# A local-attention block: scores behind the value corners, and a new order of work on VectorE

## The chip, the cores and the metric

The kernel runs on one core of a Trainium2 chip, in one launch. The core has TensorE (PE: matmuls into PSUM, eight banks of 512 floats for each of 128 partitions), VectorE (DVE), ScalarE (ACT), GpSimd (POOL), and SyncE (SP), which here issues all DMAs. The engines run side by side, each through its own list of instructions in order, and meet at semaphores. The metric is the device time of one execution in microseconds (us), lower is better. Before the change it is 3746.49 us, the median of three runs (3743.70 to 3751.31).

## The reference

The input x is 8 sequences of 1024 rows of 256 floats. The result is x + A(xn) + F(xn), where xn is x normalised by row, A is a linear attention with a Taylor feature map, and F is a two-layer transformer with local attention. Cut to what matters for F:

```python
for l in range(2):
    h = shift_token(x)                 # second half of the columns comes from the row before
    q, k, v = split(h @ wqkv[l])       # 8 heads of 64
    q = rotary(l2norm(q) * qs); k = rotary(l2norm(k) * ks)
    sim = 8 * q @ k.T                  # blocks of 128 queries, their own 128 keys and the 128 before
    sim = where(i < j or i > j + 128, -max, sim)
    x = x + (softmax(sim) @ v) @ wo[l]
    h = layernorm(shift_token(x)) * lg + lb
    a, g = split(h @ w1[l] + b1[l])
    x = x + (a * gelu(g)) @ w2[l] + b2[l]
```

## The kernel before

The kernel has two parts. `taylor_block` computes xn and A and stores them; it is not changed. `transformer_block`, from about 1020 us on, computes F and adds the rest.

**Tiles and steps.** The 8 sequences are two streams of four. A step is one tile of 128 rows of one stream in one layer. The attention of a tile needs the tile before it in the same stream and layer, so the kernel goes through 32 rounds in which four steps, two streams by two layers, follow each other: 128 steps in 132 slots, and a few more slots to empty the pipeline.

**The slot.** Each engine runs the same sequence of calls, `slot(nxt, cur, att, nrm, ffn)`, once per slot, in which five neighbouring steps stand at five stages: `nxt` gets its rows transposed (`x_T`, `copy_hT`), `cur` is projected to K, Q and V, rotated and transposed, `att` has its attention, `nrm` has its residual x1, its layer norm and the transpose of the result (`hn_T`, `copy_hnT`), and `ffn` goes through the feed-forward (`up`, gelus, `gated`, `down`, `add_ffn`). A step moves on by one stage with each slot. The order within a slot is written out by hand for each engine, and that is what the change edits.

**PE's slot before** (`slot`, line 1458): scores of `att` (lines 1364 and 1371), K and Q of `cur` (1339), `up` (1443, 1448), V (1339), `prob_T` (1382, 1386), `down` (1455), `attend` (values of the middle 1401, of the corners 1411), `heads_T` for K and for Q (1344), `x_T` (1331, 1332), `hn_T` (1427), `out_project` (1420). Scores and corners use 64x64 tiles of the array, the middle values 128x64, all else full 128 wide ones.

**DVE's slot before** (line 1169): `add_attention` (1120, x1 from PSUM), four times `mask_scores` (1091 adds the mask and takes the maximum of a head, 1098 scales the maxima of two), `row_statistics` (1125 on x1, 1127 on its shifted half, 1130, 1132), `normalise` of four heads (1105 reciprocal, 1108 one scaling for each head), `cosines` of K (1058), `normalise` of the other four, `squares` of K (1066, 1068), `gated` (1154, six gates, of which `down` needs two to begin), `rotate` K (1075), `layer_norm` (1137, 1138), `cosines`, `squares` and `rotate` of Q, `unit_k` (1081), `add_ffn` (1161, 1167), `set_mask` (1050), `copy_hnT` (1144).

**The others, whose work is not changed except for one move on ACT.** ACT: exponentials of three pairs of heads (1258), copy of K (1225), the fourth pair, square of K (1233), copy and square of Q, gelus (1280, 1283, with a table load), copy of V (1240), `copy_pT` (1266), a table load back for the exponential (1307), `copy_oT` (1271), `copy_kT` (1247), `copy_qT` (1252), `copy_hT` (1217, 1220). POOL: `ln_root` (985) for `nrm`, behind the variance of 1132; then `turn` (997), two multiplications for K and two for Q; then the roots `norm_k` (1004) and `norm_q` (1011) behind the squares; and in every second slot `residual` (1016, 1019). SP: `shift` (900, 901: the second half of x1, one row down, into `xsh`, which 1127 waits for), every second slot a load, `keep_k` (906), `carry` (926), residual loads (894, 895), `place_v` (918, 919), `store` (931), `keep_v` (911 to 913).

**PSUM.** Banks are shared by hand: scores use banks 0 to 3, and XT, HNT, OT and DOWN are the banks of the transposed rows, of the transposed norm, of attention's output (two from OT on) and of the result of `down`.

Of the kernel before, what the change touches and what calls it, by code (L numbers as in the profile page):

```python
# [681 lines left out]
def transformer_block(nc, PAIRS, x, xn_d, attn_d, wqkv_s, wo, w1, b1, w2, ln, qk_scale, rotary, masks, ident, out):  # L682
# [6 lines left out]
    with ExitStack() as ctx:  # L689
# [12 lines left out]
        ps = ctx.enter_context(nc.psum_tensor("f_ps", [P, 8, 512], F32))  # L702

        SCORES = (0, 1, 2, 3)
        XT, HNT, K, V, Q, KT, QT, OT, WO, DOWN = 2, 3, 4, 5, 5, 4, 5, 0, 7, 6
        UP = (6, 7, 4)

        wo_s = sb("fwo_s", [P, LAYERS, INNER // P, DIM])
# [82 lines left out]
        k_cosd = sem("k_cosd")  # L791
# [243 lines left out]
        def _(dve):  # L1035
# [34 lines left out]
            def rotate(step, a, cosd, turned_by, done):  # L1070
                n, s, l, it = step
                heads = slice(a * HEADS, a * HEADS + HEADS)
                dve.wait_ge(cosd, n + 1)
                dve.wait_ge(turned_by, 2 * n + 2)
                v.tensor_tensor(qk[:, heads, :], cosine[:, heads, :], turned[:, heads, :], ALU.add).then_inc(done, 1)
# [8 lines left out]
            def mask_scores(step, p):  # L1084
                n, s, l, it = step
                heads = PAIRS_OF_HEADS[p]
                both_heads = slice(heads[0], heads[1] + 1, 2)
                dve.wait_ge(score_ps, 4 * n + p + 1)
                dve.sem_inc(passed_dve, 1)
                for k, h in enumerate(heads):  # L1090
                    last = v.tensor_tensor_reduce(out=chances(h), in0=ps[:, SCORES[p], k * 256:k * 256 + BAND],  # L1091
                                                  in1=mask[s][l][:, HALF - k * HALF:HALF - k * HALF + BAND],
                                                  scale=1.0, scalar=-3.0e38, op0=ALU.add, op1=ALU.max, accum_out=nmax[:, h:h + 1])
                last.then_inc(masked, 1)
                dve.wait_ge(masked, 4 * n + p + 1)
                if p == 0:
                    dve.wait_ge(qnorm_ready, n + 1)
                v.scalar_tensor_tensor(nmax[:, both_heads], nmax[:, both_heads], -1.0, rnorm[:, both_heads],  # L1098
                                       ALU.mult, ALU.mult).then_inc(nmax_ready, 1)

            def normalise(step, q):
                n, s, l, it = step
                four = slice(4 * q, 4 * q + 4)
                dve.wait_ge(exped, 4 * n + 2 * q + 2)
                v.reciprocal(rsum[:, four], psum[:, four]).then_inc(rsum_ready, 1)
                dve.wait_ge(rsum_ready, 2 * n + q + 1)
                for h in range(4 * q, 4 * q + 4):
                    last = v.tensor_scalar_mul(chances(h), chances(h), rsum[:, h:h + 1])  # L1108
                    if h % 2:
                        last.then_inc(prob, 1)  # L1110
# [58 lines left out]
            def slot(nxt, cur, att, nrm, ffn):  # L1169
                if nrm:  # L1170
                    add_attention(nrm)
                if att:
                    for p in range(4):
                        mask_scores(att, p)
                if nrm:
                    row_statistics(nrm)
                if att:
                    normalise(att, 0)
                if cur:
                    cosines(cur, 1, k_ready, k_cosd)  # L1180
                if att:
                    normalise(att, 1)
                if cur:
                    squares(cur, 1, sqk_ready, knorm_ready, ssqk_sum, ssqk_ready)
                if ffn:
                    gated(ffn)
                if cur:
                    rotate(cur, 1, k_cosd, k_turned, k_rotated)
                if nrm:
                    layer_norm(nrm)  # L1190
                if cur:
                    cosines(cur, 0, q_ready, q_cosd)
                if cur:
                    squares(cur, 0, sqq_ready, qnorm_ready, ssqq_sum, ssqq_ready)
                    rotate(cur, 0, q_cosd, q_turned, q_rotated)
                if cur:
                    unit_k(cur)
                if ffn:
                    add_ffn(ffn)
                if nxt:  # L1200
                    set_mask(nxt)
                if nrm:
                    copy_hnT(nrm)

# [3 lines left out]
        def _(act):  # L1208
# [79 lines left out]
            def slot(nxt, cur, att, nrm, ffn):  # L1288
                if att:
                    for p in range(3):  # L1290
                        exps(att, p)
                if cur:
                    copy_part(cur, 1, K, k_ps, k_ready)
                if att:
                    exps(att, 3)
                if cur:
                    square(cur, 1, k_ready, ssqk_sum, sqk_ready)
                    copy_part(cur, 0, Q, q_ps, q_ready)
                    square(cur, 0, q_ready, ssqq_sum, sqq_ready)
                if ffn:  # L1300
                    gelus(ffn)
                if cur:
                    copy_v(cur)
                if att:
                    copy_pT(att)
                if cur:
                    a.activation(primed_s[:, :], mhalf[:, 0:1], ACT.Exp)
                if att:
                    copy_oT(att)
                if cur:  # L1310
                    copy_kT(cur)
                    copy_qT(cur)
                if nxt:
                    copy_hT(nxt)

# [3 lines left out]
        def _(pe):  # L1319
# [25 lines left out]
                              qk[:, i * HEADS + h:i * HEADS + h + 2, :].rearrange("p h d -> p (h d)"), id_s[:, :])  # L1345
                last.then_inc(done, 1)

            def scores(step, cur, ffn, p):
                n, s, l, it = step
                if p == 0:  # L1350
                    pe.wait_ge(kT_ready, n + 1)
                    pe.wait_ge(qT_ready, n + 1)
                if p == 2 and cur:
                    pe.wait_ge(hT_ready, cur[0] + 1)
                if p == 2 and ffn:
                    pe.wait_ge(hnT_ready, ffn[0] + 1)
                for k in range(2):
                    middle, corner = k * 256 + k * HALF, k * 256 + (1 - k) * P
                    for q in (p, p + 1):
                        h = PAIRS_OF_HEADS[q][k]  # L1360
                        r = slice(h % 2 * HD, h % 2 * HD + HD)
                        for half in range(2):
                            rows = slice(half * HALF, half * HALF + HALF)
                            mm(ps[rows, SCORES[q], middle:middle + P], qT[r, h // 2, rows], kT[s][l][r, h // 2, HALF:HALF + P],  # L1364
                               start=True, stop=True)
                    for q in (p, p + 1):
                        h = PAIRS_OF_HEADS[q][k]
                        r = slice(h % 2 * HD, h % 2 * HD + HD)
                        for half in range(2):
                            rows = slice(half * HALF, half * HALF + HALF)  # L1370
                            last = mm(ps[rows, SCORES[q], corner:corner + HALF], qT[r, h // 2, rows],  # L1371
                                      kT[s][l][r, h // 2, half * BAND:half * BAND + HALF], start=True, stop=True)
                        if k == 1:
                            last.then_inc(score_ps, 1)
# [81 lines left out]
                last.then_inc(down_ps, 1)  # L1456

            def slot(nxt, cur, att, nrm, ffn):
                if att:
                    for p in (0, 2):  # L1460
                        scores(att, cur, ffn, p)
                if cur:
                    project(cur, 1, K, k_ps)
                    project(cur, 0, Q, q_ps)
                if ffn:
                    up(ffn, cur, nrm)
                if cur:
                    pe.wait_ge(q_ready, cur[0] + 1)
                    project(cur, 2, V, v_ps)
                if att:  # L1470
                    prob_T(att)
                if ffn:
                    down(ffn)
                if att:
                    if nrm and not ffn:
                        pe.wait_ge(x1_ready, nrm[0] + 1)
                    attend(att)
                if cur:
                    pe.wait_ge(k_unit, cur[0] + 1)
                    heads_T(cur, 1, KT, kT_ps)  # L1480
                    pe.wait_ge(v_ready, cur[0] + 1)
                    pe.wait_ge(q_rotated, cur[0] + 1)
                    heads_T(cur, 0, QT, qT_ps)
                if nxt:
                    x_T(nxt)
                if nrm:
                    hn_T(nrm)
                if att:
                    out_project(att)
# [100 lines left out]
```

## Time and profile before

| | |
|---|---|
| median of 3 runs | 3746.49 us |
| the profiled execution | 3746.68 us, its span 3744.5 us |
| PE busy | 3532.4 us, 94% |
| DVE busy | 2620.1 us, 70% |
| ACT busy | 2688.9 us, 72% |
| POOL busy | 1197.5 us, 32% |
| mean granted TensorE clock | 0.973 |

The span is the time from the first to the last instruction of the program. An engine is busy while an instruction of its own runs; issuing DMAs and waiting are not counted. Matmuls are pipelined, so two that follow each other overlap in their rows: what one costs is seen from start to start. In the view of time (the timeline) neighbouring instructions of one line are one row with their count, a bracket tells the idle time of the engine before it and who ended it.

### The profile page before, as it was taken

How to read it: one execution, taken by the hardware profiler on the slowest of the kernel's cores; microseconds unless marked ns; L12 is line 12 of the kernel's file. 1: busy time of each engine (PE TensorE's matmuls, PEld its weight loads, DVE VectorE, ACT ScalarE, POOL GpSimd, SP SyncE). 2: the span in 40 equal slices, each digit the busy share in tenths (PEclk: the TensorE clock that was granted, in tenths of full speed). 3: DMA queues.
4: the chain of work that ended last, by engine and by line, in shares of the span. 5: the costliest groups of instructions: out<-in, count | busy, mean ns of one | idle time of the engine just before them, and what ended most of it. 6: DMA issues, size and time to landing. Idle time of an engine off the chain costs nothing.

```text
span 3744.5 us, 88007 instructions
## 1 busy us (share of the span) xinstructions
PE 3532.4 (94%) x32736; PEld 2444.0 (65%) x32736; DVE 2620.1 (70%) x8128; ACT 2688.9 (72%) x5852; POOL 1197.5 (32%) x1191
## 2 busy tenths in 40 slices
PE   7988998889659999999999999999999999999997
PEld 3333333333247777777777777777777777777786
DVE  3554555455448787787878777787878787777874
ACT  5777777777537777777777777777777777777774
POOL 2111111111133343333334343333334343333332
PEclk9999999899879999999999999999999999999999
DMA  6535554455332222222222222222222222222210
GB/s 166 119 77 96 119 119 83 89 120 108 56 122 53 70 58 64 59 65 64 58 66 60 66 55 70 61 61 65 60 67 55 70 58 64 58 67 64 58 53 21
DMA packets 269210, 277.31 MB, mean 74 GB/s; under 512 B 38768, under 2 KB 202864, under 8 KB 268144
## 3 DMA queue, kind: packets, MB, share of 16 engines
q1 hardware_dynamic: 268784, 271.68, 30.6%
q8 instruction: 261, 4.28, 0.5%
q14 instruction: 165, 1.35, 0.1%
HBM read 97.23 MB, written 50.33 MB: 39 GB/s over the span
## 4 chain that ended last, share of the span: by engine, by line
PE 51%; DVE 10%; issue 5%; SPq 2%; DMA 2%; POOL 1%; ACT 0%; DVEq 0%; POOLq 0%
PE f_ps L1339 13%; PE f_ps L1443 11%; PE f_ps L1455 6%; PE f_ps L1420 5%; PE f_ps L1344 3%; PE f_ps L1364 3%; DVE pr L1108 3%; PE f_ps L1401 2%; PE f_ps L1382 2%; PE f_ps L1411 2%; DVE cosine L1058 1%; PE f_ps L1371 1%; DMA xsh<-x 1%; DVE act_u L1154 1%; DVE ssq L1066 1%
## 5 line engine op out<-in xcount | busy, mean ns | idle before, releaser
L1258 ACT ACTIVATE pr<-pr,nmax,rnorm 128x192 f32<-128x192 f32 x1024 | 546.0, 535 | 346.5 <-DVE nmax L1098 346.5
L1339 PE MATMUL f_ps<-wqkv_s,hT 128*128 128x512 f32 x1536 | 718.7, 604 | 11.6 <-ACT hT L1220 6.2
L520 ACT ACTIVATE weights<-t_ps,four_s 128x1024 f32<-128x1024 f32 x576 | 584.4, 1185 | 108.5 <-PE t_ps L628 108.0
L1443 PEld LDWEIGHTS f_ps<-hnT,w_s 128*128 128x128 f32 x5120 | 593.9, 193 | 60.3 <-issue 58.8
L1443 PE MATMUL f_ps<-hnT,w_s 128*128 128x128 f32 x5120 | 595.4, 276 | 0.8 <-DVE hnT L1144 0.8
L1108 DVE TENSOR_SCALAR pr<-pr,rsum 128x192 f32<-128x192 f32 x1024 | 448.0, 498 | 9.0
L1339 PEld LDWEIGHTS f_ps<-wqkv_s,hT 128*128 128x128 f32 x1536 | 273.3, 191 | 271.3 <-issue 246.6
L985 POOL TENSOR_TENSOR rstd<-ve,f_mhalf 128x1 f32<-128x1 f32 x128 | 81.5, 637 | 1117.7 <-DVE ve L1132 1117.7
L383 DVE SCALAR_TENSOR_TENSOR weights<-weights,causal_s 128x512 f32<-128x512 f32 x192 | 176.7, 937 | 345.8 <-ACT weights L520 345.8
L628 PE MATMUL t_ps<-qkT 96*128 96x512 bf16 (+3 forms) x1536 | 326.4, 346 | 93.0 <-DMA qkT<-parts_dram 85.1
L997 POOL TENSOR_TENSOR turned<-qk,rot 128x256 f32<-128x256 f32 x512 | 395.2, 797 | 56.4 <-ACT qk L1225 42.8
L1091 DVE CUSTOM_DVE_ANT_0 pr<-f_ps,mask 128x192 f32<-128x192 f32 x1024 | 326.3, 355 | 68.1 <-PE f_ps L1371 66.1
L628 PEld LDWEIGHTS t_ps<-qkT 96*128 96x128 bf16 x1536 | 119.1, 100 | 368.7 <-ACT weights L520 185.0
L1455 PE MATMUL f_ps<-w_s,act_u 128*128 128x256 f32 x1536 | 353.7, 380 | 1.8 <-DVE act_u L1154 1.7
L1011 POOL TENSOR_TENSOR rnorm<-ssq,f_mhalf 128x8 f32<-128x8 f32 x128 | 248.2, 1939 | 298.9 <-DVE ssq L1068 298.9
L645 PE MATMUL t_ps<-weights,vals 128*32 128x512 f32 (+3 forms) x3072 | 324.6, 519 | 10.7 <-DVE weights L383 10.7
L1455 PEld LDWEIGHTS f_ps<-w_s,act_u 128*128 128x128 f32 x1536 | 282.1, 190 | 37.0 <-DVE act_u L1154 3.7
L1004 POOL TENSOR_TENSOR rnorm<-ssq,f_mhalf 128x8 f32<-128x8 f32 x128 | 210.6, 1645 | 199.3 <-DVE ssq L1068 199.3
L1271 ACT ACTIVATE oT<-f_ps 128x512 f32<-128x512 f32 x128 | 76.5, 598 | 251.4 <-PE f_ps L1411 251.4
L1144 DVE TENSOR_SCALAR hnT<-f_ps,ln_s 128x128 f32<-128x128 f32 x256 | 93.3, 406 | 225.3 <-PE f_ps L1427 225.3
L277 POOL TENSOR_TENSOR yT<-yT,den 128x1024 f32<-128x1024 f32 x24 | 58.1, 2423 | 600.8 <-DVE den L326 600.8
L1420 PE MATMUL f_ps<-fwo_s,oT 128*128 128x256 f32 x1024 | 242.8, 380 | 1.6 <-ACT oT L1271 1.4
(122 smaller groups left out, 6493.6 us busy)
## 6 DMA issues: line engine op xcount, KB each, us to landing
vw<-vw SPq DMA_DIRECT2D x628, 128.0 KB, 2.4
qkT<-parts_dram SPq DMA_DIRECT2D x384, 128.0 KB, 5.8
kT<-kT SPq DMA_DIRECT2D x124, 256.0 KB, 2.6
parts_dram<-parts SPq DMA_DIRECT2D x64, 384.0 KB, 3.2
xs<-x_dram SPq DMA_DIRECT2D x8, 1024.0 KB, 7.9
xn_dram<-xn SPq DMA_DIRECT2D x8, 1024.0 KB, 5.3
attn_dram<-ao SPq DMA_DIRECT2D x8, 1024.0 KB, 10.1
xin<-xn_dram SPq DMA_DIRECT2D x64, 128.0 KB, 2.2
```

The costliest lines, as they stand in the source:

```text
L520: a.activation(weights[:, w:w + 2, :], ps[:, bank:bank + 2, :], ACT.Square, bias=four_s[:, :]).then_inc(squared, 1)
L628: last = mm(ps[:, unit_bank(n) + k, o:o + 512 - c], qkT[g % 2][:, 1, h, j * P:(j + 1) * P], qkT[g % 2][:, 0, h, half * 512 + c:(half + 1) ...
L645: last = mm(ps[h * VP:(h + 1) * VP, half, c:512], vals[:, j, g * GH + h, :], weights[:, GH * (i % RING) + h, o:o + 512 - c], start=(j == 0 ...
L997: g.tensor_tensor(turned[:, heads, f], qk[:, heads, z], sines, ALU.mult).then_inc(done, 1)
L1011: g.tensor_tensor(rnorm[:, :HEADS], ssq[:, :HEADS], mhalf[:, :HEADS], ALU.pow).then_inc(qnorm_ready, 1)
L1091: last = v.tensor_tensor_reduce(out=chances(h), in0=ps[:, SCORES[p], k * 256:k * 256 + BAND], in1=mask[s][l][:, HALF - k * HALF:HALF - k * ...
L1108: last = v.tensor_scalar_mul(chances(h), chances(h), rsum[:, h:h + 1])
L1258: last = a.activation(chances(h), chances(h), ACT.Exp, bias=nmax[:, h:h + 1], scale=rnorm[:, h:h + 1], accum_out=psum[:, h:h + 1])
L1339: last = mm(ps[:, b, :], rows, wqkv_s[:, l, c, i * INNER:(i + 1) * INNER], start=(c == 0), stop=(c == KC - 1))
L1420: last = mm(ps[:, WO, 0:DIM], oT[:, c, :], wo_s[:, l, c, :], start=(c == 0), stop=(c == INNER // P - 1))
L1443: last = mm(ps[:, UP[j // 2], o:o + P], w1_s[:, l, c, half * FULL + j * P:half * FULL + j * P + P], hnT[:, c, :], start=(c == 0), stop=(c ...
L1455: last = mm(ps[:, DOWN, 0:DIM], act_u[:, j, :], w2_s[:, l, j, :], start=(j == 0), stop=(j == FB - 1))
```

## The change

PE: `scores` moves from the head of the slot after to the end of its own, right behind `attend`, and works on `cur`. `heads_T` for K and Q moves ahead of `attend`, right behind `down`. ACT: `copy_kT` and `copy_qT` move ahead of the table load and `copy_oT`. DVE: the four `mask_scores` move from the head of the slot after to the end of their own, between `set_mask` and `copy_hnT`; the scaling of the first four heads moves ahead of `row_statistics`; `cosines` and `squares` of Q, `rotate` of K and `layer_norm` move ahead of `gated`. Four results move to other PSUM banks, with two waits to fit: Q waits for `hnT_ready`, the third pair of scores for `x2_ready`. The diff, cut to its core:

```diff
-        XT, HNT, K, V, Q, KT, QT, OT, WO, DOWN = 2, 3, 4, 5, 5, 4, 5, 0, 7, 6
+        XT, HNT, K, V, Q, KT, QT, OT, WO, DOWN = 4, 5, 4, 5, 5, 4, 5, 6, 7, 3
@@ DVE slot
                 if nrm:
                     add_attention(nrm)
                 if att:
-                    for p in range(4):
-                        mask_scores(att, p)
+                    normalise(att, 0)
                 if nrm:
                     row_statistics(nrm)
-                if att:
-                    normalise(att, 0)
                 if cur:
                     cosines(cur, 1, k_ready, k_cosd)
                 if att:
                     normalise(att, 1)
                 if cur:
                     squares(cur, 1, sqk_ready, knorm_ready, ssqk_sum, ssqk_ready)
+                    cosines(cur, 0, q_ready, q_cosd)
+                    squares(cur, 0, sqq_ready, qnorm_ready, ssqq_sum, ssqq_ready)
+                    rotate(cur, 1, k_cosd, k_turned, k_rotated)
+                if nrm:
+                    layer_norm(nrm)
                 if ffn:
                     gated(ffn)
                 if cur:
-                    rotate(cur, 1, k_cosd, k_turned, k_rotated)
-                if nrm:
-                    layer_norm(nrm)
-                if cur:
-                    cosines(cur, 0, q_ready, q_cosd)
-                if cur:
-                    squares(cur, 0, sqq_ready, qnorm_ready, ssqq_sum, ssqq_ready)
                     rotate(cur, 0, q_cosd, q_turned, q_rotated)
-                if cur:
                     unit_k(cur)
                 if ffn:
                     add_ffn(ffn)
                 if nxt:
                     set_mask(nxt)
+                if cur:
+                    for p in range(4):
+                        mask_scores(cur, p)
                 if nrm:
                     copy_hnT(nrm)
@@ ACT slot
                 if cur:
+                    copy_kT(cur)
+                    copy_qT(cur)
                     a.activation(primed_s[:, :], mhalf[:, 0:1], ACT.Exp)
                 if att:
                     copy_oT(att)
-                if cur:
-                    copy_kT(cur)
-                    copy_qT(cur)
@@ PE scores
-                if p == 2 and cur:
-                    pe.wait_ge(hT_ready, cur[0] + 1)
+                if p == 0 and not att and some(n):
+                    pe.wait_ge(pT_ready, 3 * n)
                 if p == 2 and ffn:
-                    pe.wait_ge(hnT_ready, ffn[0] + 1)
+                    pe.wait_ge(x2_ready, ffn[0] + 1)
@@ PE slot
-                if att:
-                    for p in (0, 2):
-                        scores(att, cur, ffn, p)
                 if cur:
                     project(cur, 1, K, k_ps)
+                    if ffn:
+                        pe.wait_ge(hnT_ready, ffn[0] + 1)
                     project(cur, 0, Q, q_ps)
...
                 if ffn:
                     down(ffn)
-                if att:
-                    if nrm and not ffn:
-                        pe.wait_ge(x1_ready, nrm[0] + 1)
-                    attend(att)
                 if cur:
                     pe.wait_ge(k_unit, cur[0] + 1)
                     heads_T(cur, 1, KT, kT_ps)
                     pe.wait_ge(v_ready, cur[0] + 1)
                     pe.wait_ge(q_rotated, cur[0] + 1)
                     heads_T(cur, 0, QT, qT_ps)
+                if att:
+                    if nrm and not ffn:
+                        pe.wait_ge(x1_ready, nrm[0] + 1)
+                    attend(att)
+                if cur:
+                    for p in (0, 2):
+                        scores(cur, att, ffn, p)
```

## Rows read from the trace of the kernel before

**Rows 1.** Windows: stretch, length, busy us (count) by engine, clock, DMA share, GB/s.
```profile
1160.00:3660.00 2500.00, 2495.96 (x25833) 1971.55 (x25826) 1981.68 (x6822) 1861.96 (x4625) 957.35 (x970) 1.00 0.23 62
```

**Rows 2.** Timeline of PE over one slot: start us, length us, what, count.
```profile
2515.54 0.45 PE L1364 MATMUL f_ps<-kT,qT 64*64 64x128 f32 x8
...
2516.81 0.29 PE L1371 MATMUL f_ps<-kT,qT 64*64 64x64 f32 x8
2517.04 3.70 PE L1339 MATMUL f_ps<-wqkv_s,hT 128*128 128x512 f32 x8
...
2528.50 2.76 PE L1455 MATMUL f_ps<-w_s,act_u 128*128 128x256 f32 x12
2531.19 1.10 PE L1401 MATMUL f_ps<-pT,vw 128*64 128x128 f32 x16
2532.21 0.70 PE L1411 MATMUL f_ps<-pT,vw 64*64 64x64 f32 x32
2532.84 1.09 PE L1344 MATMUL f_ps<-f_id,qk 128*128 128x128 f32 x8
...
2536.03 0.45 PE L1364 MATMUL f_ps<-kT,qT 64*64 64x128 f32 x8
```

**Rows 3.** Timeline of PE while the pipeline fills and drains.
```profile
1076.23 3.60 PE L1339 MATMUL f_ps<-wqkv_s,hT 128*128 128x512 f32 x8
...
1149.72 3.53 PE L1339 MATMUL f_ps<-wqkv_s,hT 128*128 128x512 f32 x4 [2.65 <-ACT qk L1225]
...
3654.09 2.86 PE L1455 MATMUL f_ps<-w_s,act_u 128*128 128x256 f32 x12 [0.37 <-DVE act_u L1154]
```

**Rows 4.** Timeline of DVE in the same slot.
```profile
2515.72 0.42 DVE L1120 TENSOR_TENSOR x<-f_ps,xmid 128x256 f32<-128x256 f32 x1 [1.07 <-PE f_ps L1420]
2516.62 0.36 DVE L1091 CUSTOM_DVE_ANT_0 pr<-f_ps,mask 128x192 f32<-128x192 f32 x1 [0.48 <-PE f_ps L1371]
...
2519.90 0.29 DVE L1125 BATCH_NORM_STATS2 st<-x 128x6 f32<-128x128 f32 x1
2520.10 0.27 DVE L1127 BATCH_NORM_STATS2 st<-xsh 128x6 f32<-128x128 f32 x1
...
2520.84 0.17 DVE L1105 RECIPROCAL rsum<-psum 128x4 f32<-128x4 f32 x1
2521.04 2.04 DVE L1108 TENSOR_SCALAR pr<-pr,rsum 128x192 f32<-128x192 f32 x4
...
2525.47 0.67 DVE L1066 TENSOR_REDUCE ssq<-sq 128x8 f32<-128x512 f32 x1
...
2526.25 1.63 DVE L1154 SCALAR_TENSOR_TENSOR act_u<-f_ps,b_s,act_u 128x128 f32<-128x128 f32 x6
2527.81 0.67 DVE L1075 TENSOR_TENSOR qk<-cosine,turned 128x512 f32<-128x512 f32 x1
2528.41 0.33 DVE L1137 TENSOR_SCALAR hn<-x,mv,rstd 128x128 f32<-128x128 f32 x1
...
2528.92 0.67 DVE L1058 TENSOR_TENSOR cosine<-qk,rot 128x512 f32<-128x512 f32 x1
```

**Rows 5.** Timeline of DVE in three other slots.
```profile
2377.48 0.29 DVE L1127 BATCH_NORM_STATS2 st<-xsh 128x6 f32<-128x128 f32 x1 [1.60 <-DMA xsh<-x]
...
2534.41 0.73 DVE L1144 TENSOR_SCALAR hnT<-f_ps,ln_s 128x128 f32<-128x128 f32 x2 [2.27 <-PE f_ps L1427]
...
3650.64 1.01 DVE L1108 TENSOR_SCALAR pr<-pr,rsum 128x192 f32<-128x192 f32 x4
```

**Rows 6.** Timeline of SP: the first shift DMA of that first slot.
```profile
2374.42 0.59 SPq L900 DMA_DIRECT2D xsh<-x  x1
```

**Rows 7.** Timeline of POOL in the slot of rows 4.
```profile
2521.00 0.63 POOL L985 TENSOR_TENSOR rstd<-ve,f_mhalf 128x1 f32<-128x1 f32 x1 [8.35 <-DVE ve L1132]
2521.52 1.44 POOL L997 TENSOR_TENSOR turned<-qk,rot 128x256 f32<-128x256 f32 x2
...
2526.49 1.64 POOL L1004 TENSOR_TENSOR rnorm<-ssq,f_mhalf 128x8 f32<-128x8 f32 x1 [1.53 <-DVE ssq L1068]
```

More of the change, by code:

```diff
@@ L1346, in heads_T, with scores @@
                 last.then_inc(done, 1)
-            def scores(step, cur, ffn, p):
+            def scores(step, att, ffn, p):
                 n, s, l, it = step
```

## The prediction

> **What bounds the kernel now.** I read the windows first, then the timelines of TensorE (PE), VectorE (DVE), GpSimd (POOL) and SP over one slot. From 1160 to 3660 us PE is busy 2495.96 of 2500 us at a granted clock of 1.00 [rows 1]: 122 slots in which nothing but PE's own work counts. One slot lasts 2536.03 - 2515.54 = 20.49 us [rows 2]. DVE is busy 1981.68 us there, 16.2 per slot, ScalarE 15.3, POOL 7.8: each has room, none waits for itself. So the change can win only in PE's own stream, and can lose by making a chain through DVE longer than a slot. Both are worked out per slot and taken 122 times against the profiled execution (3746.68 us, 0.2 over the median of 3746.49).
>
> **PE's own stream.** The matmuls stay the same. What goes is one change of array shape, from full 128-wide tiles to 64-wide ones and back: before, attention values and scores each stood alone; now scores follow the value corners, both on 64x64 tiles. Into narrow tiles: 12 matmuls of the down projection hand over after 2.69 us, and at their spacing of 0.216 they would after 2.60 (their 2.76 is 11 spacings and one length of 0.38): 0.09. Out again: the last corner group hands over after 2517.04 - 2516.81 = 0.23 where the three before it take 0.11, so 0.12; and K and Q's eight matmuls take 3.70 behind scores, 3.60 in the one slot where they follow full tiles [rows 2, 3]: 0.10. Together 0.31: PE alone would need 20.49 - 0.31 = 20.18 us.
> The Trainium skill (TensorEngine Tiling, Tiling Modes) states that switching the tiling mode drains TensorE. The 0.31 agrees with that; by this rule alone the kernel would be faster, which is the first rival below.
>
> **The new loop.** Before, masks and maxima of a step came at the start of the next slot, far from anything that PE waited for in it: the gates stood early in DVE's order and "down" found them ready. Now everything is in one ring: scores -> masks -> hnT copy -> x1 -> statistics, softmax scaling, squares, rotation, layer norm -> gates -> down -> transposes -> values -> next scores. I add it up from the first score matmul, time 0.
>
> 1. First mask at 2516.62 - 2515.54 = 1.08; eight masks with maxima take 3.28 to the next instruction, 3.36 with the last short one whole [rows 2, 4]: 4.44. (POOL's root for q, which the first maximum now needs, is issued some 5 us before this.)
> 2. copy_hnT now comes behind the masks: two in 0.73, start to start 0.65 [rows 5]: 5.09. PE wants hnT before Q. K ends 15.08 - 11.36 + 1.72 = 5.44 after the first score (2517.04 to 2528.50 less the 0.10; half of K and Q's 3.43), so this is just hidden. x1 takes 0.42 [rows 4]: 5.51. Scaling of the first four heads, free of POOL, and the first statistic follow: 0.34 + 0.20 + 0.94 + 0.20: DVE stands at the second statistic at 6.77.
> 3. That one needs the half of x1 shifted by a DMA. Before, the masks lay over this DMA. Where the first of the two is issued at 2374.42, the statistic starts at 2377.48 [rows 5, 6]: 3.06; in the quickest slots it is 2.6. SP should be free to issue at once (its last work of a slot, keep_v, waits only for the values and ends some 3 us earlier). 5.51 + 0.03 + 3.06 = 8.60: a new wait of 1.8 us. Bounds: 8.1 and, by the longest issue-to-landing of 3.7 us on that line, 9.8.
> 4. Statistics to the next instruction 2520.84 - 2520.10 = 0.74 [rows 4]: 9.34. The variance is out 0.08 later, at 9.42; POOL starts its root 0.08 behind (0.63 long, 0.52 to the next) and only then the turns of K and Q, four multiplications of 0.70 start to start (two take 1.44) [rows 7]: 10.02 to 12.85. K and Q have long been copied, so the four run together.
> 5. DVE: cosines of K 0.60 (as long as the rotation, 0.67, and taken at its 0.60 to the next), reciprocal 0.20: at 10.14 the second four scalings start, right into these turns. Four scalings alone take 1.01; beside two turns 2.04 [rows 4, 5]. In the trace each scaling that meets a turn ends 0.12 us after that turn does; beside four turns they all end with the last: the next instruction starts at 12.89, where it would be 11.08 without POOL. Price 1.81. Bounds: 0 (never met) and about 2.1 (0.52 for each turn).
> 6. Squares of K 0.78, cosines of Q 0.60, squares of Q 0.78, rotation of K 0.60, layer norm 0.51 [rows 4]: 16.16. Four of these stood behind the gates before. Two gates: 0.26 to the second's start and 0.34: 16.76. PE follows 0.06 later: 16.82.
> 7. PE: down 2.60, 0.10 for the restart after a wait (2.86 against 2.76) [rows 2, 3], transposes 0.87 with 0.09 to narrow tiles, values 1.02 and corners 0.63 less the 0.11 that leaving cost [rows 2]: 5.20. Next scores at 22.02.
>
> PE alone would be at "down" at 20.18 less these 5.10 (without the restart) = 15.08. So it stands 1.7 us in each slot, before "down", and the gain of 0.31 is inside this wait. A slot takes 22.0 us, 1.5 more than 20.49. Sum: 3746.7 + 122 x 1.49 = 3928. The slots of filling and draining are left as they are: there PE already waits 5 us for DVE's rotation, and the new order shortens one wait and lengthens another; 5 us either way.
>
> **What I cost at nothing.** Rotation of Q and unit_k end at 16.16 + 1.55 + 0.61 + 0.69 = 19.0, the transposes of K want them at 19.5: hidden, and 0.5 is all the room. add_ffn and set_mask end at 20.3, before the third score pair. copy_kT and copy_qT (0.60 each, one after the other as the transposes end) are done some 0.7 us before scores; if ScalarE were late, scores would be too. Its exponentials start behind copy_hT, at 2.4, and the first four are ready at 4.6, before DVE asks at 5.4. copy_oT now waits behind a table load (1.28) but ends at about 1.3, before the output projection wants it (2.0). The bank changes (XT, HNT, OT, DOWN) only move waits: x2_ready before the third score pair is met 2 us early. SP's order is unchanged; keep_k, issued in the same place, finds its scores done.
>
> **A rule weighed.** The trace shows scalings held up by turns, but the rotation of K at 2527.81, beside POOL's root of 2526.49, took 0.67 and was not [rows 4, 7]. The Trainium skill (SBUF — State Buffer, Who interferes with whom) states an exclusive lock: a Vector instruction with two SBUF inputs contends with any GpSimd instruction that reads SBUF. Taken literally the cosines of Q, which now lie beside the root of K, would wait up to its 1.64 us, and the slot would be 23.7; the row speaks against that, and I take nothing for it.
>
> **Rivals.**
> *PE keeps the bound, faster.* If scalings don't meet the turns, or POOL gives way, step 5 costs nothing and the loop is 22.02 - 1.81 = 20.21, no more than PE's 20.18. Then the gain of one pair of shape changes is real: 122 x 0.3 = 37, 3710 us. For it: both loops are so near each other that 1.8 us decide. Against: root and scalings hang on the same statistic, 0.1 us apart, so that they meet in every slot. It decides where DVE's loop is below 20.49. Chance 0.10.
> *Half of it.* The DMA lands in 2.6 and two of the four scalings slip past: 22.02 - 0.45 - 0.9 = 20.7 us, 3746.7 + 122 x 0.2 = 3770; with one of the two 3805 to 3870. Chance 0.20.
> *The clock falls.* PE would stand 1.7 us in each slot. In the fill of the pipeline, after a wait of 2.65 us, four matmuls took 3.53 us instead of 1.88 [rows 3], at a granted clock of about 0.5. Waits of 0.9 us and less passed without. If the new wait did this over step 7, it would add up to 1.7 us to a slot: 23.7, or 4135 us; in every second slot 4030. For it: slots in which the DMA is late have a wait of 2.5. Chance 0.12.
> *The forecast*, DVE's ring at 21.6 to 22.5 us a slot, 3880 to 3990: chance 0.58.
>
> **How the numbers follow.** Low end: 3800, which leaves out the faster case and part of the half case; high end 4040, half the clock case. Faster by over 0.2% (7.5 us, about what can be told from no change) 0.12: the first rival and a little for an order of DVE that I have costed too dear. Within 0.2%: 0.04, since a loop would have to fall on 20.49 by chance. Slower 0.84.
>
> **What would show it.** Right: "down" (the w2 matmuls) has an idle time of 1 to 2 us before it in each slot, released by DVE's gate; the second statistic waits 1 to 2.5 us for the shifted half in all slots, not in every second; the second four scalings take about 2.8 us and lie over four turns in a row; PE's busy share in the steady part falls to 92%; the stretch from corners to scores has no gap of the kind shown. Wrong: slots of 20.2 us with PE unbroken; the shifted half in time; turns that start before the scalings; the transposes of K, not "down", as the place where PE waits (then the ring runs over unit_k); or a granted clock below 1.00 in the steady part.

## The result and the profile after

| | before | after |
|---|---|---|
| median (us) | 3745.09 (3741.94 to 3751.31) | 3926.74 (3921.52 to 3930.52) |
| ratio, 95% interval | | 1.0485 (1.0472 to 1.0497) |
| span of the profiled execution | 3744.5 | 3919.4 |
| PE busy | 3532.4, 94% | 3548.4, 91% |
| mean from one "down" to the next | 20.54 | 21.88 |

The change costs 4.85%; 3928 us was forecast. "Down" starts 128 times in each trace, so its starts divide the span into the fill up to the third, 120 slots up to the 123rd, and the drain. Before, these two stand at 1172.61 and 3637.83 us, after at:

```profile
1182.39 2.86 PE L1451 MATMUL f_ps<-w_s,act_u 128*128 128x256 f32 x12 [1.04 <-DVE act_u L1154]
...
3807.39 2.86 PE L1451 MATMUL f_ps<-w_s,act_u 128*128 128x256 f32 x12 [0.84 <-DVE act_u L1154]
```

The span is 174.9 us longer: 159.8 of it in the 120 slots ((3807.39 - 1182.39) - (3637.83 - 1172.61)), 9.8 in the fill, 5.3 in the drain.

The windows of the steady part, with the columns of [rows 1]. PE, which was idle for 4 of 2500 us there, is now busy 94% of the time (92% was forecast):

```profile
1300.00:3740.00 2440.00, 2301.07 (x23588) 1817.97 (x23587) 1836.40 (x6242) 1716.69 (x4241) 928.13 (x895) 0.99 0.22 59
```

The page's chain of work that ended last, by engine. Before the change PE had 51% of it and DVE 10%:

```profile
DVE 37%; PE 16%; issue 10%; DMA 7%; SPq 2%; POOL 1%; DVEq 0%; POOLq 0%; ACT 0%; ACTq 0%
```

The view of waits from 1250 to 3800 us, which holds 117 slots (us in all, times, the longest one):

```profile
DVE pr L1091 <- PE f_ps L1367: 334.5, 117, 3.1
DVE st L1127 <- DMA xsh<-x: 178.9, 117, 3.1
...
PE f_ps L1451 <- DVE act_u L1154: 131.8, 116, 2.7
```

The first is DVE with nothing to do until the next scores: it is idle nearly 3 us in each slot and still sets the pace, because it is one link of a ring and not because it is full. The second is the wait for the shifted half, 1.53 us a slot, which came in about every second slot before. It is 1.27 in most slots and up to 3.1 in those where the DMA is late. The third is PE ahead of "down", 1.14 a slot.

PE's timeline over one slot, to be laid beside [rows 2]:

```profile
2506.12 0.40 PE L1360 MATMUL f_ps<-kT,qT 64*64 64x128 f32 x8
...
2520.88 0.60 PE L1382 MATMUL f_ps<-f_id,pr 128*128 128x128 f32 x4
2522.95 2.86 PE L1451 MATMUL f_ps<-w_s,act_u 128*128 128x256 f32 x12 [1.48 <-DVE act_u L1154]
2525.65 1.04 PE L1340 MATMUL f_ps<-f_id,qk 128*128 128x128 f32 x8
2526.61 1.09 PE L1397 MATMUL f_ps<-pT,vw 128*64 128x128 f32 x16
2527.64 0.69 PE L1407 MATMUL f_ps<-pT,vw 64*64 64x64 f32 x32
2528.16 0.40 PE L1360 MATMUL f_ps<-kT,qT 64*64 64x128 f32 x8
```

DVE and POOL in that slot, which answer to [rows 4, 5, 7]:

```profile
2507.16 0.36 DVE L1091 CUSTOM_DVE_ANT_0 pr<-f_ps,mask 128x192 f32<-128x192 f32 x1 [3.12 <-PE f_ps L1367]
...
2510.79 0.72 DVE L1144 TENSOR_SCALAR hnT<-f_ps,ln_s 128x128 f32<-128x128 f32 x2
2511.43 0.41 DVE L1120 TENSOR_TENSOR x<-f_ps,xin 128x256 f32<-128x256 f32 x1
...
2511.96 1.01 DVE L1108 TENSOR_SCALAR pr<-pr,rsum 128x192 f32<-128x192 f32 x4
...
2514.89 0.29 DVE L1127 BATCH_NORM_STATS2 st<-xsh 128x6 f32<-128x128 f32 x1 [1.72 <-DMA xsh<-x]
...
2516.51 2.50 DVE L1108 TENSOR_SCALAR pr<-pr,rsum 128x192 f32<-128x192 f32 x4
2518.94 0.67 DVE L1066 TENSOR_REDUCE ssq<-sq 128x8 f32<-128x512 f32 x1
...
2522.30 1.63 DVE L1154 SCALAR_TENSOR_TENSOR act_u<-f_ps,b_s,act_u 128x128 f32<-128x128 f32 x6
```

```profile
2515.80 1.06 POOL L985 TENSOR_TENSOR rstd<-ve,f_mhalf 128x1 f32<-128x1 f32 x1 [12.85 <-DVE ve L1132]
2516.78 2.82 POOL L997 TENSOR_TENSOR turned<-qk,rot 128x256 f32<-128x256 f32 x4
```

The whole ring is to be seen here; times count from its scores at 2506.12. Masks at 1.04, hnT at 4.67, then x1, a wait of 1.72 for the DMA, statistics, and four scalings that last 2.50 because four turns lie over them, where the four before them, alone, took 1.01. Gates at 16.18, "down" at 16.83 after PE has been idle for 1.48, next scores at 22.04. PE's own share is what runs without a bracket: the corners pass into scores with no gap.

### The profile page after: what moved, and what is told of

The parts are those of the page before. It is cut to its first block, busy times and chain, and to the rows that moved or that the text cites. A ratio compares the mean times of both kernels' runs of the same rounds, so it can differ in the third digit from the quotient of the medians.

```text
span 3919.4 us, 88008 instructions
## 1 busy us (share of the span) xinstructions
PE 3548.4 (91%) x32736; PEld 2460.9 (63%) x32736; DVE 2642.0 (67%) x8128; ACT 2700.3 (69%) x5852; POOL 1251.1 (32%) x1191
## 4 chain that ended last, share of the span: by engine, by line
DVE 37%; PE 16%; issue 10%; DMA 7%; SPq 2%; POOL 1%; DVEq 0%; POOLq 0%; ACT 0%; ACTq 0%
DVE pr L1091 7%; DVE pr L1108 7%; DMA xsh<-x 7%; PE f_ps L1451 5%; DVE ssq L1066 4%; PE f_ps L1397 3%; PE f_ps L1340 3%; DVE act_u L1154 3%; DVE qk L1075 2%; DVE cosine L1058 2%; DVE hnT L1144 2%; PE f_ps L1407 2%; DVE qk L1081 2%; SPq L900 2%; PE f_ps L1360 1%
## 5 line engine op out<-in xcount | busy, mean ns | idle before, releaser
L1335 PE MATMUL f_ps<-wqkv_s,hT 128*128 128x512 f32 x1536 | 705.2, 595 | 9.9 <-ACT hT L1217 5.9
L985 POOL TENSOR_TENSOR rstd<-ve,f_mhalf 128x1 f32<-128x1 f32 x128 | 133.7, 1044 | 1725.6 <-DVE ve L1132 1725.6
L1439 PE MATMUL f_ps<-hnT,w_s 128*128 128x128 f32 x5120 | 597.8, 276 | 10.2 <-DVE hnT L1144 10.2
L1451 PE MATMUL f_ps<-w_s,act_u 128*128 128x256 f32 x1536 | 379.2, 398 | 136.9 <-DVE act_u L1154 136.9
L1335 PEld LDWEIGHTS f_ps<-wqkv_s,hT 128*128 128x128 f32 x1536 | 281.3, 191 | 269.8 <-issue 188.5
L1108 DVE TENSOR_SCALAR pr<-pr,rsum 128x192 f32<-128x192 f32 x1024 | 442.7, 495 | 9.0
L1244 ACT ACTIVATE kT<-f_ps 128x512 f32<-128x512 f32 x128 | 76.5, 597 | 516.1 <-PE f_ps L1340 516.1
L1451 PEld LDWEIGHTS f_ps<-w_s,act_u 128*128 128x128 f32 x1536 | 290.6, 196 | 203.0 <-DVE act_u L1154 166.1
L997 POOL TENSOR_TENSOR turned<-qk,rot 128x256 f32<-128x256 f32 x512 | 367.6, 747 | 22.8 <-DMA w_s<-w_dram 13.0
L1277 ACT ACTIVATE act_u<-f_ps,b_s 128x128 f32<-128x128 f32 x640 | 204.3, 365 | 114.5 <-PE f_ps L1444 89.9
L1004 POOL TENSOR_TENSOR rnorm<-ssq,f_mhalf 128x8 f32<-128x8 f32 x128 | 252.6, 1974 | 47.0 <-DVE ssq L1068 47.0
L1154 DVE SCALAR_TENSOR_TENSOR act_u<-f_ps,b_s,act_u 128x128 f32<-128x128 f32 (+1 forms) x768 | 209.2, 341 | 16.8 <-ACT act_u L1277 13.4
```

Of the source, the lines that this page charges most:

```text
L997: g.tensor_tensor(turned[:, heads, f], qk[:, heads, z], sines, ALU.mult).then_inc(done, 1)
L1004: g.tensor_tensor(rnorm[:, HEADS:], ssq[:, HEADS:], mhalf[:, HEADS:], ALU.pow).then_inc(knorm_ready, 1)
L1154: v.scalar_tensor_tensor(act_u[0:rows, j, :], ps[0:rows, UP[j // 2], (j % 2) * 256:(j % 2) * 256 + P], b1_s[0:rows, l, 0, j:j + 1], act_u[ ...
L1335: last = mm(ps[:, b, :], rows, wqkv_s[:, l, c, i * INNER:(i + 1) * INNER], start=(c == 0), stop=(c == KC - 1))
L1439: last = mm(ps[:, UP[j // 2], o:o + P], w1_s[:, l, c, half * FULL + j * P:half * FULL + j * P + P], hnT[:, c, :], start=(c == 0), stop=(c ...
L1451: last = mm(ps[:, DOWN, 0:DIM], act_u[:, j, :], w2_s[:, l, j, :], start=(j == 0), stop=(j == FB - 1))
```

## The experiments

All are compared with the kernel before on the same chip (3746.88 us in the session of e1 to e4, 3747.61 in that of the rest). The last column is the mean from one "down" to the next, from the third to the 123rd, in the profiled execution. Where a text below says what happens in most slots or on average, it is counted over the slots between 1250 and 3600 us.

| kernel | median us | ratio, 95% interval | slot us |
|---|---|---|---|
| after, turns ahead of the root (e1) | 3769.96 | 1.0062 (1.0047 to 1.0077) | 20.67 |
| after, statistics late (e2) | 3721.52 | 0.9929 (0.9913 to 0.9946) | 20.19 |
| after, statistics of the unshifted half (e3) | 3718.40 | 0.9921 (0.9906 to 0.9936) | 20.25 |
| PE's part alone (e4) | 3932.71 | 1.0494 (1.0478 to 1.0510) | 21.98 |
| before, turns ahead of the root (e5) | 3736.89 | 0.9973 (0.9963 to 0.9983) | 20.49 |
| e1 and e2 together (e6) | 3738.31 | 0.9976 (0.9967 to 0.9985) | 20.38 |
| DVE's part alone (e7) | 3876.87 | 1.0348 (1.0334 to 1.0362) | 21.63 |
| after, residual early (e8) | 3891.28 | 1.0376 (1.0362 to 1.0391) | 21.56 |

### e1: the price of scalings beside turns

```diff
@@ POOL slot of after
-                if nrm:
-                    ln_root(nrm)
                 if cur:
                     turn(cur, 1, k_ready, k_rotated, k_turned)
                     turn(cur, 0, q_ready, q_rotated, q_turned)
+                if nrm:
+                    ln_root(nrm)
+                if cur:
                     norm_k(cur)
```

> The changed kernel with one move on POOL: the turns of K and Q ahead of the layer norm's root, so that they no longer start with the second four scalings. My theory (the meeting of turns and scalings costs the ring 1.8 us a slot, beside the wait for the shifted half of 1.5): the ring falls from 21.9 us to about 20.2, PE's own 20.18 becomes the bound, idle before 'down' is near 0, time 3715 to 3735. Rival (the meeting is hidden behind something, the wait for the shifted half alone makes the ring): 3915 to 3930. Second rival (the turns only meet other two-input work on DVE instead, cosines or rotation): 3770 to 3850.

It came out at 3769.96: 157 us of the 182 come back with nothing changed in the orders of DVE, PE and the DMAs. The slot is 1.21 us shorter. DVE's timeline, and POOL's below it, show what is left in a common slot:

```profile
2516.99 0.95 DVE L1059 TENSOR_TENSOR cosine<-qk,rot 128x512 f32<-128x512 f32 x1
...
2518.06 1.27 DVE L1109 TENSOR_SCALAR pr<-pr,rsum 128x192 f32<-128x192 f32 x4
```

```profile
2516.65 1.87 POOL L997 TENSOR_TENSOR turned<-qk,rot 128x256 f32<-128x256 f32 x2 [0.64 <-ACT qk L1223]
```

and in one of four slots of 113 in which the cosines bear nearly all of it:

```profile
2536.44 0.29 DVE L1128 BATCH_NORM_STATS2 st<-xsh 128x6 f32<-128x128 f32 x1 [1.28 <-DMA xsh<-x]
...
2537.60 1.27 DVE L1059 TENSOR_TENSOR cosine<-qk,rot 128x512 f32<-128x512 f32 x1 [0.32 <-issue]
...
2538.99 1.01 DVE L1109 TENSOR_SCALAR pr<-pr,rsum 128x192 f32<-128x192 f32 x4
```

```profile
2534.86 1.42 POOL L997 TENSOR_TENSOR turned<-qk,rot 128x256 f32<-128x256 f32 x2 [10.93 <-ACT qk L1223]
2536.91 1.41 POOL L997 TENSOR_TENSOR turned<-qk,rot 128x256 f32<-128x256 f32 x2 [0.63 <-ACT qk L1223]
```

The second four scalings take 1.18 on average, where they took 2.51, and the wait for the DMA is still there. But the turns of Q now lie over the end of the cosines of K or the first scaling: the cosines take 0.90 on average instead of 0.69. So 0.38 us a slot of the price is left, part of it with a new payer. PE still waits 0.13 a slot before "down", and 0.23 in every second slot before the transposes of K (e8 is about that one). The time is 35 us above the upper end of what was expected and falls on the lower end of the second rival, whose mechanism is there in part. The price of meeting is confirmed; its removal is not whole.

### e2: no wait for the shifted half

```diff
@@ DVE slot of after
                     normalise(att, 0)
-                if nrm:
-                    row_statistics(nrm)
                 if cur:
                     cosines(cur, 1, k_ready, k_cosd)
                 if att:
                     normalise(att, 1)
+                if nrm:
+                    row_statistics(nrm)
```

> The changed kernel with one move on DVE: row_statistics behind the cosines of K and the second four scalings. Theory: the scalings and cosines cover the shift DMA, and POOL's root and turns start only when the scalings are done, so both prices go (1.5 and 1.8 us of 21.9); the turns then meet the cosines of Q and hold up the rotation of K by up to 1.5 us. Ring at most 20.3, PE bound, 3715 to 3745. Rival (the rotation of K, waiting for late turns, takes the place of what was removed): 3800 to 3860.

3721.52 us, faster than after and than before, and the fastest kernel here that leaves nothing out. In the windows PE is bound again:

```profile
1300.00:3550.00 2250.00, 2248.80 (x23595) 1809.79 (x23595) 1786.69 (x6234) 1713.43 (x4231) 968.22 (x896) 1.00 0.24 63
```

and an undisturbed slot, "down" to "down", is 20.14 us long where it was 20.49:

```profile
1264.96 2.76 PE L1451 MATMUL f_ps<-w_s,act_u 128*128 128x256 f32 x12
...
1285.10 2.76 PE L1451 MATMUL f_ps<-w_s,act_u 128*128 128x256 f32 x12
```

So PE's new order, with one pair of shape changes fewer, is worth 0.35, and the forecast's 0.31 was nearly that. No run changes the shapes alone. Both prices are gone with one move, as the timelines of DVE and POOL show in a slot where the DMA was late:

```profile
2509.19 1.01 DVE L1108 TENSOR_SCALAR pr<-pr,rsum 128x192 f32<-128x192 f32 x4
...
2510.78 0.29 DVE L1127 BATCH_NORM_STATS2 st<-xsh 128x6 f32<-128x128 f32 x1 [0.37 <-DMA xsh<-x]
...
2512.27 0.70 DVE L1068 TENSOR_SCALAR ssq<-ssq 128x8 f32<-128x8 f32 x1
2512.88 0.68 DVE L1058 TENSOR_TENSOR cosine<-qk,rot 128x512 f32<-128x512 f32 x1
...
2515.38 0.76 DVE L1137 TENSOR_SCALAR hn<-x,mv,rstd 128x128 f32<-128x128 f32 x1
```

```profile
2512.22 3.84 POOL L997 TENSOR_TENSOR turned<-qk,rot 128x256 f32<-128x256 f32 x4
```

The variance now comes after the scalings, POOL's root and turns hang on it, and so they can't meet the scalings. They meet three small operations (0.70 and 0.76 instead of 0.17 and 0.34), which costs some 1.5 us that the ring has to spare. The gain is 0.36 x 120 = 43 us in the slots; the fill is 11.8 us longer and the drain 6.6, and 25 remain.

### e3: the DMA's price alone

```diff
@@ row_statistics of after; layer_norm takes over the wait for the shift
-                dve.wait_ge(shifted[s][l], 32 * it + 32)
-                v.bn_stats(st[:, 1, :], xsh[s][l][:, :]).then_inc(stats, 1)
+                v.bn_stats(st[:, 1, :], x1[s][l][:, P:DIM]).then_inc(stats, 1)
```

This leaves the shift by one row out of the mean and the variance.

> The changed kernel, in which the second statistic is taken of the unshifted half of x1, so that it doesn't wait for the DMA (this leaves the shift out of the statistics; the layer norm still uses the shifted half and waits for it, long landed). Theory: the wait of 1.5 us a slot goes and nothing else moves, since root, turns and scalings all follow the same statistic: ring 20.4 us, 3735 to 3760. Rival (scalings meet the turns differently and K or Q is not yet copied when the turns could start, so half is lost again): 3780 to 3850. Rival (the DMA wait is only slack before the turns): 3915 to 3930.

3718.40, 17 us under the lower end of what was expected. The scalings are held up as much as in after, seen on DVE and on POOL:

```profile
2506.48 2.51 DVE L1108 TENSOR_SCALAR pr<-pr,rsum 128x192 f32<-128x192 f32 x4
```

```profile
2506.75 2.83 POOL L997 TENSOR_TENSOR turned<-qk,rot 128x256 f32<-128x256 f32 x4
```

and yet PE is busy 2248.74 of 2250 us. Without the wait of 1.54 the ring is at about 20.3 (21.88 - 1.54), close enough to PE's 20.14 to vanish nearly whole. So neither price is the cause by itself: with both the ring is longer than PE's slot, and taking away one of them is nearly enough.

### e4 and e7: the two parts of the change alone

e4 keeps PE, ACT and the banks of after and puts DVE back into the order of before. e7 is the kernel before with the four calls ahead of the gates:

```diff
@@ e7, DVE slot of before
                     squares(cur, 1, sqk_ready, knorm_ready, ssqk_sum, ssqk_ready)
-                if ffn:
-                    gated(ffn)
                 if cur:
+                    cosines(cur, 0, q_ready, q_cosd)
+                    squares(cur, 0, sqq_ready, qnorm_ready, ssqq_sum, ssqq_ready)
                     rotate(cur, 1, k_cosd, k_turned, k_rotated)
                 if nrm:
                     layer_norm(nrm)
+                if ffn:
+                    gated(ffn)
                 if cur:
-                    cosines(cur, 0, q_ready, q_cosd)
-                if cur:
-                    squares(cur, 0, sqq_ready, qnorm_ready, ssqq_sum, ssqq_ready)
                     rotate(cur, 0, q_cosd, q_turned, q_rotated)
```

> PE's, ACT's and the bank part of the change alone, with DVE in its order of before (x1, masks of att, statistics, scalings, squares of K, gates, rotation and norm, then Q). By rows: x1 4.0 us after the first score, masks to 7.6, gates at 13.4 to 14 and so in time for 'down' at 15.1, but unit_k ends at 18.8 where the transposes of K, now right behind 'down', want it at 17.8: slot 21.3 us, PE waits before the transposes and not before 'down', 3800 to 3880. Rival (DVE's order alone made the loss, PE's part brings the shape gain of 0.3 us a slot): 3700 to 3715.

> The kernel before with one part of the new DVE order: cosines and squares of Q, rotation of K and layer norm ahead of the gates (scores, masks, banks, transposes as before). Theory (where the gates stand decides): 2.5 us of work ahead of them moves them from 11.3 to 13.8 behind the first score, 'down' waits 1.5 us in a slot, slot 21.9 to 22.1, 3915 to 3945. Rival (only the ring through scores and masks is long; the gates alone have slack): 3740 to 3760.

e4, 3932.71 us, is as slow as the whole change, but PE stands elsewhere. Its timeline:

```profile
2497.95 2.76 PE L1454 MATMUL f_ps<-w_s,act_u 128*128 128x256 f32 x12
2502.22 1.09 PE L1343 MATMUL f_ps<-f_id,qk 128*128 128x128 f32 x8 [1.52 <-DVE qk L1081]
```

"Down" is on time and the transposes of K wait 1.58 us a slot for unit_k, which ends DVE's list. The place was forecast and the size was not (3880 was the upper end): I had the end of unit_k at 18.8 us of the slot and it came at 19.3. e7, 3876.87, has it the other way round, in PE's timeline:

```profile
2513.71 0.60 PE L1385 MATMUL f_ps<-f_id,pr 128*128 128x128 f32 x4
2515.12 2.86 PE L1454 MATMUL f_ps<-w_s,act_u 128*128 128x256 f32 x12 [0.81 <-DVE act_u L1154]
```

It waits 0.87 before "down" on average, not 1.5, and the slot of 21.63 is some 0.4 us shorter than expected, the time 38 us under the lower end. One thing that the expectation left out: in the longer slot the shift's DMA is always on time (1.1 us of waits in 103 slots, 52.5 in before). Neither part gains by itself, and together they gain only with e2's move: PE's order wants unit_k early, the new DVE order gives it that (its end at 18.95, where e4 has 19.3) and pays with late gates. No run has e2's move with one part alone.

### e5, e6 and e8: controls and what is left

e5 is e1's edit made in the kernel before; e6 has e1's and e2's edits in after; e8:

```diff
@@ POOL slot of after
+                if nrm and nrm[2] == 1:
+                    residual(nrm)
                 if nrm:
                     ln_root(nrm)
...
                     norm_q(cur)
-                if nrm and nrm[2] == 1:
-                    residual(nrm)
```

> Control: the kernel before with POOL's turns ahead of the layer norm's root, the same move as e1_turns_first. There PE sets the slot with 20.49 us and DVE is not in its way, so nothing should move: 3740 to 3752, ratio 0.998 to 1.002. If it moved by a per cent, e1 would have shown a merit of POOL's order and not the price of the new ring.

> The changed kernel with both moves: statistics behind the second scalings (e2) and POOL's turns ahead of the root (e1). e2 already has PE as the bound (20.13 us a slot), so the second move has nothing to give: 3717 to 3726, as e2, if the gains don't add. If they did add it would be below 3710. A loss against e2 (above 3735) would say that early turns meet the scalings, which e2 had moved clear of them.

> The changed kernel with POOL's two residual additions moved from the end of its slot to the head. In the profile of after they lie over the rotation of Q and unit_k, which take 1.01 and 1.21 us instead of 0.67, and PE waits 0.22 us for unit_k in every second slot. At the head they meet the first scalings, which the wait for the shifted half covers. Theory: 0.1 to 0.2 us a slot less on the mean, 3900 to 3918. Rival (the additions hold up the scalings or the root by more than the wait covers): 3925 to 3960.

e5 was to change nothing (3740 to 3752 us) and gained 0.27%: its mean slot is 20.49 against 20.54 before. So the kernel before was bound by PE to within 0.05 us a slot, not wholly. Meeting turns cost before almost as much DVE time as after (448.0 and 442.7 us busy at the line of the scalings, by the pages' groups), but there it lay in slack.

e6 is slower than e2 alone, and over the 3735 that its expectation named for a loss: with the turns free of the root they start early again and lie over the second four scalings, on DVE:

```profile
2515.34 2.51 DVE L1109 TENSOR_SCALAR pr<-pr,rsum 128x192 f32<-128x192 f32 x4
...
2523.64 1.01 DVE L1076 TENSOR_TENSOR qk<-cosine,turned 128x512 f32<-128x512 f32 x1
2524.57 1.21 DVE L1082 TENSOR_TENSOR qk<-qk,rnorm 128x512 f32<-128x512 f32 x1
```

Everything behind is late, and in every second slot PE waits 0.20 us for unit_k. Two cures of one trouble are worse than one of them.

The last two of these rows are what e8 tests. In every second slot POOL's residual additions lie over rotation of Q and unit_k; moved to the head of POOL's slot, the first of the two still lies over the rotation (1.01), the second meets the first scalings (1.56 for four), unit_k takes 0.68 us in all slots, and the slot is 0.32 shorter, more than the 0.1 to 0.2 expected. In after, "down" to the transposes of K commonly takes 2.70 us from start to start in one half of the slots and 3.09 in the other; in e8 it is 2.69 in both. That is 0.20 of the 0.32. About 0.08 more is the clock (below), which fell in two slots and not in eight, at 1.6 us each.

## Why the prediction was right

Its steps were right in kind, each within 0.5 us, and 3928 against 3926.74 is luck: errors nearly cancel, one of them a slip in its own sum (below). Means over 111 slots of after, time 0 at the first score matmul:

| step | forecast | measured |
|---|---|---|
| 1 first mask | 1.08 | 1.04 |
| 2 hnT copy starts; x1 written | 4.44; 5.51 | 4.34; 5.40 |
| 3 second statistic; its wait | 8.60; 1.8 | 8.27; 1.54 |
| 4 POOL's root; turns | 9.50; 10.02 to 12.85 | 9.19; 10.15 to 12.98 |
| 5 second four scalings end; their time | 12.89; 2.8 | 12.41; 2.50 |
| 6 gates; "down" | 16.16; 16.82 | 15.69; 16.35 |
| 7 unit_k ends; transposes of K | 19.0; 19.5 | 18.95; 19.36 |
| next scores | 22.02 | 21.90 |

**Steps 1 and 2** hold to 0.1. **Step 3** has the wait 0.26 too long, as the statistic starts 2.83 us after the DMA's issue and not 3.06; the bounds of 8.1 to 9.8 hold the mean (single slots have 7.96 to 9.82). **Step 4**: POOL's root took 1.06 us, where it took 0.63 in [rows 7]: the cosines of K now lie beside it. Turns began 0.13 later than forecast although the variance was out earlier. **Step 5**: so the first of the four scalings is through, at 10.22, as the turns begin; the other three end behind the first three turns, and the fourth turn (its end is at 12.98) holds nobody up. The price was 1.49 (2.50 against 1.01) and not 1.81. e1 confirms that it is these turns.

**Step 6** ends 0.47 early, so that PE waits 1.14 before "down" and not 1.7; **step 7** gives 0.35 of this back: PE needed 5.55 from "down" to scores on average, not 5.20. The slot shown above has 5.21. In every second slot 0.39 is added before the transposes of K, 0.20 on average; I had costed this at nothing with 0.5 us to spare, and the room was gone, since rotation of Q and unit_k took 1.01 and 1.21, not 0.67 and 0.68 (another slot of DVE's timeline). Another 0.12 is the clock, below.

```profile
2501.37 1.01 DVE L1075 TENSOR_TENSOR qk<-cosine,turned 128x512 f32<-128x512 f32 x1
2502.30 1.21 DVE L1081 TENSOR_TENSOR qk<-qk,rnorm 128x512 f32<-128x512 f32 x1
```

The trace of before had the residual additions behind everything that PE waited for, and I did not follow what they would lie beside once rotation of Q and unit_k moved. This is the main miss in the working of the ring.

**The rule weighed.** Beside these additions of POOL (128x256, two operands in SBUF) both DVE operations took up to 0.53 longer, and the cosines of K beside the turns in e1 took 0.25 longer in most slots and 0.58 in a few. By the Trainium skill (SBUF — State Buffer, Who interferes with whom), a Vector instruction with two SBUF inputs contends with any GpSimd instruction that reads SBUF: here the rows agree. The cosines of Q start some 0.2 us ahead of POOL's root of K (128x8) and took 0.69, about as alone; the root grew from 1.64 to 1.99, so if the two contend there, POOL pays. The rotation of K starts 1.2 us into that root and took 0.69 too. There the trace does not agree with the exclusive lock that the prediction quotes, and to take nothing for the cosines of Q was right.

**The sum.** 1.49 x 122 = 182 was forecast against 174.9 of span. But the steps' own figures are 22.02 and 20.49, which differ by 1.53: the sum should have been 187, and the forecast 3933. The slots gave 159.8 (1.33 each; before was 20.54 and not 20.49, and after 21.88 and not 22.02), fill and drain 15.1 where I had 0 with 5 either way. The profiled execution, 3921.5 us, is also 5 under the median. PE's timeline of the fill shows a wait that I had not priced: "up" behind the hnT copy, which now stands behind the masks. PE waits so for 10.2 us over the whole trace, all in fill and drain, where before it was 0.8; the rest of the 15.1 was not traced to its cause.

```profile
1094.18 6.36 PE L1439 MATMUL f_ps<-hnT,w_s 128*128 128x128 f32 x40 [2.37 <-DVE hnT L1144]
```

In a full slot K and Q cover this copy, as step 2 said; where the pipeline is half empty nothing does.

**The rivals.** *PE keeps the bound* was wrong for after, but its arithmetic was right: with both prices away (e2) or the DMA's alone (e3) the kernel is at or near PE's bound, with the turns moved (e1) within some 0.5 us of it, and PE's gain is real. *Half of it* did not happen: the quickest slot was 21.2. (Its "3805 to 3870" would be some 3824 to 3878 by its own figures.) *The clock* happened, rarely. Between 1200 and 3650 us there are eight stretches at half the full clock, 27 us in all; before has none. Each lies over a "down" that PE had waited for by 1.88 us or more; so does a ninth at 3698. Of the 14 slots with such waits five passed at the full clock, as did all with shorter ones; in e8 ten of 12 passed, with waits of up to 2.35, so the wait alone does not decide. PE's timeline and the window of one:

```profile
2187.59 0.60 PE L1382 MATMUL f_ps<-f_id,pr 128*128 128x128 f32 x4
2190.88 4.45 PE L1451 MATMUL f_ps<-w_s,act_u 128*128 128x256 f32 x12 [2.69 <-DVE act_u L1154]
```

```profile
2192.00:2194.00 2.00, 2.00 (x6) 1.58 (x5) 1.91 (x2) 0.00 (x0) 1.29 (x2) 0.50 0.00 0
```

After a wait of 2.69 us "down" ran at a granted 0.50, the 1.2 GHz level, and took 4.45 instead of 2.86. Eight times some 1.6 is 13 us of the 175. The mean wait is 1.14, and no slot of after with a wait under 1.88 saw the fall: this rival had the mechanism right and its frequency wrong.

## What to carry to other kernels

An order that shortens the bounding engine's stream closes a loop, and the loop's length, not any engine's busy share, then sets the pace: add it up from one start to the next, with each DMA and each meeting of engines in it. Here 0.35 us of real gain was lost behind two prices of 1.5 us that had cost next to nothing before, the DMA's because the masks lay over it and the turns' because DVE had slack; one call moved behind two others (statistics behind the cosines of K and the second scalings) got it back, 0.7% under the kernel before. When a call moves, look also at what it will lie beside on the other engine, in each kind of slot.

## What the runs showed of the hardware

- What DVE and POOL cost each other when they meet depends on the kind of operation. Scalings of 128x192 go from 0.25 each to the length of the turns (2.50 for four, after). Tiny ones of 128x8 go from 0.17 to 0.70 (e2). Cosines beside turns took 0.68 in e2, unharmed, and the turns there took 3.84 for four instead of 2.83; in the slot of e1 shown last the cosines took 1.27 and the turns 1.41 for two. The start times fit one reading, that the earlier of the two goes first: in e2 the cosines start 0.02 us ahead of a turn (2512.88 and 2512.90), which then takes 1.25. In e1's common slot they start in the midst of a turn (2516.99 in 2516.65 to 2517.39) and take 0.95, and the next turn, started behind them at 2517.34, takes 1.18. No run tests this, and two rows do not fit it: the rotation of K in the midst of a root (above), and in after the second of the late scalings, which starts 0.03 us ahead of a turn (2516.75 and 2516.78) and is held up until its end.
- POOL's root of one column takes 0.56 beside a reduction (e2), 0.63 beside scalings (before) and 1.06 beside the cosines (after).
- One pair of array shape changes fewer (full to 64-wide tiles and back), in PE's new order, goes with a slot of 20.14 us instead of 20.49. The Trainium skill (TensorEngine Tiling (Array Packing), Tiling Modes) states that a change of tiling mode drains TensorE, and the 0.35 agrees with it.
